# When GpSimd splits the weights of layer one's first expert: six pieces ahead without a pause, or three ahead in step with VectorE's rows

## The reference, cut to what matters

```python
h = jnp.einsum('eti,eih->eth', einp2, w_c_fc) + b_c_fc
g = jnp.einsum('eti,eih->eth', einp2, w_gate) + b_gate
o = jnp.einsum('eth,eho->eto', jax.nn.silu(h * g), w_c_proj) + b_c_proj
```

## Time and profile before

| What | us |
|---|---|
| median of three runs | 1855.84 |
| the three runs | 1855.84, 1847.66, 1855.99 |
| the profiled execution | 1852.79 |
| its span, first to last instruction | 1851.1 |
| stretch of `experts_1` up to its last step, in the span | about 1495 to 1798 |

### The profile page before, as it was taken

How to read it: one execution, slowest core, us unless ns; L and a number is a source line. 1 busy time by engine, 2 the same in 40 slices (tenths; PEclk the granted TensorE clock), 3 DMA queues, 4 the chain that set the end, 5 groups by cost and what they waited for, 6 DMA issues and landing times. The chain is left out here.

```text
span 1851.1 us, 36828 instructions
## 1 busy us (share of the span) xinstructions
PE 1644.8 (89%) x12703; PEld 1358.4 (73%) x12703; DVE 1167.7 (63%) x2713; ACT 845.5 (46%) x2455; POOL 575.1 (31%) x894
## 2 busy tenths in 40 slices
PE   6997599999998785899999579999999759999988
PEld 3665377777776574788888557777777659999986
DVE  5776467777776543477776546666666446666656
ACT  2333256555554142455555434444444235544524
POOL 2112223444442253222210022232322155444413
PEclk9999699999998898999999789999999969999999
DMA  8000323444450452000000030000000031123001
GB/s 249 0 0 1 124 69 123 129 128 127 128 153 12 154 171 94 21 14 14 16 6 1 1 110 18 18 18 18 18 9 1 1 137 69 69 91 114 1 1 40
DMA packets 87274, 114.25 MB, mean 62 GB/s; under 512 B 4788, under 2 KB 76680, under 8 KB 86888
## 3 DMA queue, kind: packets, MB, share of 16 engines
q1 hardware_dynamic: 82008, 99.56, 16.8%
q0 software_dynamic: 5136, 12.98, 2.1%
HBM read 64.68 MB, written 47.84 MB: 61 GB/s over the span
## 5 line engine op out<-in xcount | busy, mean ns | idle before, releaser
L1312 PE MATMUL ps<-e_ex_high,e_w_high 128*128 128x264 f32 x512 | 146.8, 287 | 6.4 <-POOL e_w_low L2671 6.4
L1312 PE MATMUL ps<-e_ex_high,e_w_low 128*128 128x264 f32 x512 | 146.6, 286 | 0.0
L1312 PE MATMUL ps<-e_ex_low,e_w_high 128*128 128x264 f32 x512 | 146.2, 285 | 0.0
L1027 ACT ACTIVATE c_probs<-ps,c_negmax 112x375 f32<-112x375 f32 x256 | 143.5, 581 | 2.1 <-DVE c_negmax L1126 2.1
L1224 PEld LDWEIGHTS ps<-const,c_probs 112*125 112x125 f32 x768 | 97.7, 193 | 47.8 <-DVE c_pT L1142 27.5
L1126 DVE TENSOR_REDUCE c_negmax<-ps 112x2 f32<-112x750 f32 x128 | 114.2, 934 | 25.5 <-PE ps L1255 25.5
L1224 PE MATMUL ps<-const,c_probs 112*125 112x112 f32 x768 | 115.8, 288 | 3.6 <-ACT c_probs L1027 2.4
L1924 PE MATMUL ps<-xnT,s_qkv 128*128 128x224 f32 x512 | 110.5, 365 | 4.7 <-ACT e_gate_up L1717 4.2
L1733 ACT ACTIVATE s_probs<-ps,s_negmax 112x112 f32<-112x112 f32 x256 | 86.5, 364 | 36.7 <-DVE s_negmax L1791 36.7
L1312 PEld LDWEIGHTS ps<-e_ex_high,e_w_high 128*128 128x128 f32 x512 | 97.7, 191 | 6.6 <-issue 6.6
L1924 PEld LDWEIGHTS ps<-xnT,s_qkv 128*128 128x128 f32 x512 | 94.8, 193 | 10.5 <-ACT e_gate_up L1717 5.8
(11 more groups left out here) (392 smaller groups left out, 4741.7 us busy)
## 6 DMA issues: line engine op xcount, KB each, us to landing
expert_rows<-d_zero SPq DMA_DIRECT2D x16, 2240.0 KB
c_ctx_in<-in_ctx SPq DMA_DIRECT2D x32, 375.0 KB
e_x_in<-expert_rows SPq DMA_DIRECT2D x43, 128.0 KB, 2.2
expert_rows<-e_y POOLq DMA_DIRECT2D x43, 128.0 KB, 2.1
e_w_gate_even<-in_L_ffn_w_gate SPq DMA_DIRECT2D x4, 1024.0 KB, 5.1
e_w_fc_even<-in_L_ffn_w_c_fc SPq DMA_DIRECT2D x4, 1024.0 KB, 7.3
e_w_proj_even<-in_L_ffn_w_c_proj SPq DMA_DIRECT2D x4, 1024.0 KB, 9.7
e_w_gate_odd<-in_L_ffn_w_gate SPq DMA_DIRECT2D x4, 1024.0 KB, 5.0
```

The lines of the kernel that those rows point to most:

```text
L1027: last = nc.scalar.activation(probs[:, g % 2, r, :], ps[:T, r, 0:S], ACT.Exp, bias=negmax[:, par, h:h + 1], accum_out=sums[:, par, h:h + 1])
L1312: last = nc.tensor.matmul(out, a, b, start=start and n == 0, stop=stop and n == len(pairs) - 1)
```

## The change

GpSimd's part of the first pair of experts is taken out of the loop and written out. In it, before each of pieces 3 to 7, GpSimd also waits until `hid_ready` is n-2, that is until VectorE has finished row n-3. Pieces 0 to 2 and pieces 8 to 15 have no such wait, and the loop now runs over the other three pairs. The operations and their order are the same on every engine.

```diff
             @block.gpsimd
             def _(pool):
-                with pool.Fori(0, E1 - 1, 2) as e2:
+                def split_piece(e2, n):
+                    j = n % NJ
+                    pool.wait_ge(piece_rounded, e2 * NJ + n + 1)
+                    for low, high, whole in zip(parts_of(w_low, j), parts_of(w_high, j), of_piece(n // NJ, j)):
+                        last = nc.gpsimd.tensor_tensor(low, whole, high.bitcast(F32), ALU.subtract)
+                    last.then_inc(piece_split, 1)
+
+                for n in range(2 * NJ):
+                    if 3 <= n < NJ:
+                        pool.wait_ge(hid_ready, n - 2)
+                    split_piece(0, n)
+                with pool.Fori(2, E1 - 1, 2) as e2:
                     for n in range(2 * NJ):
-                        j = n % NJ
-                        pool.wait_ge(piece_rounded, e2 * NJ + n + 1)
-                        for low, high, whole in zip(parts_of(w_low, j), parts_of(w_high, j), of_piece(n // NJ, j)):
-                            last = nc.gpsimd.tensor_tensor(low, whole, high.bitcast(F32), ALU.subtract)
-                        last.then_inc(piece_split, 1)
+                        split_piece(e2, n)
```

## The result

| | before | after |
|---|---|---|
| median, us (12 runs each) | 1855.91 | 1850.56 |
| lowest to highest | 1844.76 to 1860.56 | 1846.06 to 1854.31 |
| span of the profiled execution | 1851.1 | 1849.2 |
| stage, from the start of e_diff to the start of its last matmul | 302.4 | 294.2 |

The ratio is 0.9967, 95% interval 0.9953 to 0.9981: the changed kernel is 0.33% faster, some 6 us (the two medians differ by 5.4 us). The forecast was +0.9 us, so it had the wrong sign.

What follows compares the result with a forecast made beforehand. It took a TensorE pause, from VectorE's cast held behind GpSimd's subtractions, as what the change is about; -8.8 + 9.7 = +0.9 us gave 1853.7 profiled, 1856.7 on the median's scale, range 1846.3 to 1858.8.

Steps and rivals of the forecast that it cites:

- What the pause is, and its price: TensorE idle before out_products(0), row 0's cast held behind GpSimd's subtractions: 7.2 us waiting plus 1.6 us half-clock restart, 8.8 us.
- Part 1, the slack of rows 0 to 4: Waits before pieces 3 to 7: remove the 8.8 us pause, cost nothing while no row is held over 1.3 us.
- Part 2, the second stretch: After the waits, GpSimd runs pieces 7 to 12 in one go: 18 subtractions, 12.4 us, from 1524.0 to 1536.4.
- The stretch of pieces 7 to 12 is like the former, so I take the hold as the likelier: Row 5's cast, asking at 1527.1, would be held until GpSimd's new stretch ends; a gain not excluded.
- the whole term of +9.7 us: Loss at row 5: TensorE idles 7.9 to 8.2 us, then restarts for 1.6 us; 9.5 to 9.8 us in all.
- one hold of ten losses in a row against ten turns won in eleven: VectorE lost ten turns to GpSimd at the cast of 1506.48, but won ten of eleven meetings in the c_cn loop.
- B: Rival: VectorE gets its turn after one subtraction in the new stretch; gain 8.8 us, 1847.0, up to 1849; chance 0.25.
- C: Rival: VectorE gets some turns, is caught in row 6 or 7; -1.4 or -3.7 us, 1854.4 or 1852.1; chance 0.18.
- D: Rival: held at row 5 with a longer half-clock restart; +1.8 us, 1857.6; chance 0.06.
- the first rival below: The prediction's pointer, from the skill page's rule, to the rival with the 8.8 us gain.
- the page's sum: By the skill page's port-lock rule, a cast waits about 0.5 us for one subtraction, so the sum is an 8.8 us gain.
- A: Rival listed first, the forecast itself: VectorE held at row 5, +0.9 us, 1856.7; chance 0.48.

Runs made afterwards that it cites:

- one_wait: Against the changed kernel: only piece 3 waits, for row 0; stage 294.1 and 294.2 us, ratio to the kernel before 0.9993.
- first_waits_again: Second execution, against the changed kernel: no waits for rows, piece 0 waits for VectorE's e_ex_low; cast of row 0 took 1.09 us, stage 294.7 us.
- restart: Against the changed kernel: only piece 3 waits, for VectorE's join in row 0; cast of row 0 took 0.43 us, stage 294.4 us, ratio to before 0.9971.

## Why the prediction was wrong, point by point

- **What the pause is, and its price.** Right for the execution that was shown; the gain was put at 8.8 us for the profiled execution, and the stages differ by 8.2. What it missed is that this is the price of a held execution, and that only some are held. The hint was in the table of times, 1847.66 beside 1855.84, and the prediction saw it but drew no term from it: the -8.8 should have been multiplied by a share. Three executions in four held, times 8 us, is the 6 us of the first set, but the other sets gave 9 us for the changed kernel and nearly nothing for one_wait, so the match is in part luck.
- **Part 1, the slack of rows 0 to 4.** Right. Row 0 was reckoned done at 1507.66, which is 1515.0 in the second profile, whose stage began 7.3 us later; it was done at 1514.88. From step 0 on TensorE waited for no piece, the operations of probabilities() cost nothing, and the load of expert 2, issued at 1533.54, held nobody up.
- **Part 2, the second stretch.** Right in place at its start: 1524.0 and 1527.1 for the stretch and the cast of row 5, shifted by 7.3 us 1531.3 and 1534.4, measured 1531.23 and 1534.34. Its length was off: it ended at 1553.77, not at 1544, with 27 subtractions in place of 18, as the steps went on and ScalarE kept supplying pieces.
- **The step that failed: "The stretch of pieces 7 to 12 is like the former, so I take the hold as the likelier".** From it came the whole term of +9.7 us, and in both profiled executions of the changed kernel that term is nothing. VectorE asked 3 us into the stretch, not 10, and after each ask the two took turns; no cast there took over 1.05 us. The prediction had weighed one hold of ten losses in a row against ten turns won in eleven, and took the queue of ready subtractions, and the same instruction, as the likeness that decides. But a stretch of 27 made no hold, and the same cast at rows 1 to 63 was never held. What the runs point to instead is how long the stretch had run before VectorE's cast came; why even then only 6 of 10 are held stays open. With no second stall, the sum is -8.2 us against a held execution and -0.3 us against a free one.
- **The rivals.** B is what happened, with casts of 0.7 to 1.05 us; its 1847.0 would be the median only if every run of before had been held. C and D didn't occur. The prediction calls B "the first rival below" where it gives the page's sum; in its list the first is A. The Trainium skill's rule (SBUF — State Buffer, Who interferes with whom), that the second engine blocks until the first's instruction finishes, is what the trace shows in the changed kernel (the cast of row 5 ends 0.29 us after the subtraction's end). In the held executions the cast waited for ten or eleven subtractions that were issued after it, and there the measurement decides.

## What to carry to other kernels

Where a cast of VectorE that others wait for can meet GpSimd's work, don't let GpSimd run on without a rest for a long time (here 9 to 10 us) before that cast comes; in the profiled executions one wait that made it rest before then was enough. To time GpSimd's pieces behind VectorE's critical instructions all the way is better still, since each fraction of a microsecond counts where TensorE has no slack, here at seven borders. And when single runs of a kernel differ by the size of a stall seen in its profile, take more than one profile before pricing the stall: it may happen only in a share of the executions.

## What the runs showed of the hardware that was not expected

- A cast of VectorE can be passed by ten or eleven subtractions of GpSimd in a row (7.6 to 7.9 us), in the same program in some executions and not in others; it ends 0.3 us after GpSimd's last one. Cutting the stretch by two pieces cut the hold to 3.83 us.
- In a normal meeting the cast ends 0.29 us after the subtraction under way (row 5 of the changed kernel), and e_hid_low, with two inputs in SBUF, takes 1.13 in place of 0.71 us. A cast that asks just before the next subtraction begins can lose that one too: 1.05 us at 0.02 us before it (row 7 of the changed kernel) and 1.09 us at 0.06 (first_waits_again). But it needn't: 0.43 us at 0.06 in restart.
- Work in front of the changed stage, with the same code, varied by 8.5 us between executions (the stage began at 1495.2 to 1503.7). A change of 6 us in 1850 is read from the stage, not from a single span.
